# A block of self-attention, cross-attention and feed-forward: rotated heads stored with features outermost, second scores one head later

## The chip, the cores and the metric

The kernel runs on one core of one Trainium2 chip. The metric is the device time of one execution in microseconds (us), smaller is better. The times are medians of several executions; a profiled execution has its own time, which stands beside its span (first to last instruction).

## The reference

Sixteen sequences of 256 positions with 512 features pass through one block, all in float32, with 16 heads of 32 features:

```python
xn = _adaln(x, noise_emb, ln1_w, ln1_b)              # layer norm, scaled and shifted by cond
q, k, v = jnp.split(xn @ qkv_w.T, 3, axis=-1)
q, k = _rope(q...), _rope(k...)                      # halves (t1, t2) of each head's 32 features
x = x + _attn(q, k, v) @ sa_out_w.T                  # self-attention
xn = _adaln(x, noise_emb, ln2_w, ln2_b)
q = _rope(xn @ q_w.T); k = _rope(context @ k_w.T); v = context @ v_w.T
x = x + _attn(q, k, v) @ ca_out_w.T                  # cross-attention on 256 context rows
xn = _adaln(x, noise_emb, ln3_w, ln3_b)
x = x + gelu(xn @ ffn_w1.T + ffn_b1) @ ffn_w2.T + ffn_b2    # 512 -> 2048 -> 512
```

## The kernel before

**Work.** An item is one sequence in one attention layer: items 0 to 15 are the self-attention, 16 to 31 the cross-attention. An item has 16 heads, so 512 heads follow one another; after them comes the feed-forward part, which the change doesn't touch. To keep float32 accuracy every operand of a big product is split in a rounded high part (ScalarE, for weights L673) and the rest as a low part (VectorE, L817), and a product is three products (hi by hi, hi by low, low by hi), accumulated in PSUM.

**The list of steps.** `stage_order` writes one list of steps. Every engine walks through the same list in the same order and does its share of each step, so a step's place is its place on all five engines at once, SyncE's DMA issues included. A head has three places; head n begins at place 3n, item i at p = 48i. At head n stand the scores of head n, then at the second place the second scores (`weigh`) of head n - LAG, then at the third the step `total` of head n. Projections, transposes, spills and stacks for the items ahead are put at fixed places between them.

**One head.** TensorE forms the scores [query, key] (L615); VectorE takes the row maxima (L861); ScalarE takes exp with that maximum as its bias and sums each row (`total`, L744). For each group G of 8 heads ScalarE then takes the logarithm of the sums, VectorE subtracts it from the negated maxima and splits the result in two parts (`max_split`, L869 to L874), TensorE turns these (`max_turn`, L622), ScalarE copies them out of PSUM (L725), and a DMA on ScalarE's queue (`max_rows`, L734) writes them as two more rows under the stacked q. The second scores (`weigh`, L634) are formed the other way round, [key, query], over 98 rows, the last two with these constants, so that a plain exp (L758) gives weights that are already normalized. `mix` (L649) multiplies them by v, with 32 matmuls for 8 heads.

**Heads before they are used.** The projection (L605) gives 128 rows of q or k with the two halves beside each other in one PSUM bank; VectorE (L832, L836), GpSimd (L931, L932), ScalarE (`rope_high`, L719) and GpSimd (`rope_low`, L938) rotate and split them. `spill` (L994, L996) writes the high and the low part to a tensor `turned` in HBM, `stack` reads them back for four heads at a time (a quad) so that the features of high and low parts lie on the partitions: q as high, low and high once more (L1007, L1009), k as high twice and low (L1013 twice, L1015). There are six quad slots (`NQ`); a stack waits until the second scores of the slot's last quad are done (L1004). A spill waits for the stacks that read the same half of `turned` two items before.

**Other limits.** Five PSUM banks (`NS`) serve scores, second scores, turned maxima and mixes in turn; each is free when the engine named in `scores_left` has read it. Three banks serve the projections. `ctx_load` (L985) brings the context of an item of the second layer into `xT`, `ctx_split` (L713 on ScalarE, L925 on GpSimd) splits it. Weights come in 128-row chunks through four raw slots (L980).

## Time and profile before

| | |
|---|---|
| median of 3 runs | 1929.85 us (1921.75 to 1933.32) |
| profiled execution | 1925.28 us |
| its span | 1923.5 us |
| TensorE busy | 1869.4 us, 97% of the span |
| ScalarE, VectorE, GpSimd busy | 1383.3, 1294.9, 785.8 us |
| mean granted TensorE clock | 0.994 |
| DMA queue of SyncE | 304.47 MB in 304528 packets |

The attention layers fill the span up to about 1240 us, the feed-forward part the rest. Busy time says how long an engine had an instruction under way; what a change can gain is in the idle time of the engine that is always wanted, in the stretches at the lower clock, and in what each wait was ended by.

### The profile page before, as it was taken

To read this page: it belongs to the slowest core of one execution; us is meant where nothing else is said; L and a number is where in the kernel's file an instruction comes from. 1 tells how busy PE (TensorE), PEld (TensorE's weight loads), DVE (VectorE), ACT (ScalarE), POOL (GpSimd) and SP (SyncE) were. 2 spreads that over 40 slices of the span, in tenths; PEclk is the share of its full clock that TensorE was granted. 3 is DMA by queue.
4 is the path that set the end of the run, shared out by engine and by line. 5 is a ranking of instruction groups with operands and counts; after the bars stand their busy time and mean duration, and the time that the engine had idled before them with its cause. 6 is when DMAs were issued, how large, how long until landed. Compare 5 with 4: busy or idle time off the path is not lost. (4 is left out here: it accounts for less than half of the span.)

```text
span 1923.5 us, 39339 instructions
## 1 busy us (share of the span) xinstructions
PE 1869.4 (97%) x13460; PEld 1630.4 (85%) x13460; DVE 1294.9 (67%) x2250; ACT 1383.3 (72%) x3813; POOL 785.8 (41%) x818
## 2 busy tenths in 40 slices
PE   8899999999998999999999998899999999999999
PEld 7788888888877888888888886688898998989898
DVE  7766676767776677676776776446667666666754
ACT  4777777888876888888888888655666666565654
POOL 3534433443442454454454441013536354444531
PEclk9999999999998999999999999999999999999999
DMA  7666676566576778767668677343232322323130
GB/s 232 195 203 185 204 223 194 177 200 198 165 220 189 204 212 233 201 197 227 199 200 225 198 217 190 109 137 110 78 99 67 99 88 89 95 71 110 45 99 33
DMA packets 306451, 308.37 MB, mean 160 GB/s; under 512 B 21072, under 2 KB 260048, under 8 KB 306256
## 3 DMA queue, kind: packets, MB, share of 16 engines
q1 hardware_dynamic: 304528, 304.47, 53.4%
q8 instruction: 111, 1.82, 0.4%
q10 hardware_dynamic: 1728, 1.39, 0.3%
q14 instruction: 84, 0.69, 0.1%
HBM read 212.46 MB, written 92.27 MB: 158 GB/s over the span
## 5 line engine op out<-in xcount | busy, mean ns | idle before, releaser
L744 ACT ACTIVATE ps_s<-ps_s,neg_max 128x256 f32<-128x256 f32 x1024 | 452.8, 443 | 55.4 <-DVE neg_max L861 48.3
L861 DVE TENSOR_REDUCE neg_max<-ps_s 128x2 f32<-128x512 f32 x512 | 349.3, 687 | 212.8 <-PE ps_s L615 212.4
L758 ACT ACTIVATE prob<-ps_s 128x512 f32<-128x512 f32 x512 | 303.4, 593 | 137.2 <-PE ps_s L634 134.3
L634 PE MATMUL ps_s<-qT,kT 98*128 98x256 f32 x1024 | 211.6, 289 | 24.4 <-DMA qT<-max_rows 21.8
L931 POOL TENSOR_TENSOR rope_c<-rope_c,rope_s 128x256 f32<-128x256 f32 x128 | 98.4, 769 | 330.5 <-DVE rope_s L836 330.5
L615 PE MATMUL ps_s<-kT,qT 96*128 96x256 f32 x1024 | 216.5, 293 | 10.7 <-ACT ps_s L744 8.3
L615 PEld LDWEIGHTS ps_s<-kT,qT 96*128 96x128 f32 x1024 | 169.9, 190 | 60.3 <-ACT ps_s L744 28.4
L605 PE MATMUL ps_g<-xx_hi,w_hi 128*128 128x256 f32 x1024 | 208.1, 285 | 1.4 <-issue 1.4
L634 PEld LDWEIGHTS ps_s<-qT,kT 98*128 98x128 f32 x1024 | 169.3, 191 | 46.9 <-issue 21.0
L744 ACT ACTIVATION_READ_ACCUMULATOR ps_s<-ps_s,neg_max 128x1 f32 x1024 | 207.8, 203 | 0.0
L605 PE MATMUL ps_g<-xx_lo,w_hi 128*128 128x256 f32 x1024 | 205.5, 282 | 0.0
L605 PE MATMUL ps_g<-xx_hi,w_lo 128*128 128x256 f32 x1024 | 205.4, 282 | 0.0
L1297 PE MATMUL ps_y<-w_hi,h_hi 128*128 128x512 f32 x512 | 201.4, 393 | 1.2 <-DVE h_lo L1422 1.2
L1297 PE MATMUL ps_y<-w_lo,h_hi 128*128 128x512 f32 x512 | 200.7, 392 | 0.0
L1297 PE MATMUL ps_y<-w_hi,h_lo 128*128 128x512 f32 x512 | 199.3, 389 | 0.0
L1422 DVE TENSOR_TENSOR h_lo<-h_sb,h_hi 128x512 fp32r<-128x512 f32 x128 | 111.1, 872 | 104.9 <-ACT h_hi L1320 103.6
L938 POOL TENSOR_TENSOR rot_lo<-rope_c,rot_hi 128x512 fp32r<-128x512 f32 x128 | 165.6, 1295 | 16.8 <-ACT rot_hi L719 14.9
L919 POOL TENSOR_TENSOR xx_lo<-xT,xx_hi 128x512 fp32r<-128x512 f32 x66 | 86.9, 1318 | 207.3 <-ACT xx_hi L705 207.2
L1281 PE MATMUL ps_h<-xf_hi,cw_hi 128*128 128x256 f32 x592 | 167.5, 283 | 0.0
L1281 PE MATMUL ps_h<-xf_lo,cw_hi 128*128 128x256 f32 x592 | 165.8, 280 | 0.0
L1281 PE MATMUL ps_h<-xf_hi,cw_lo 128*128 128x256 f32 x592 | 165.7, 280 | 0.0
L605 PEld LDWEIGHTS ps_g<-xx_hi,w_hi 128*128 128x128 f32 x1024 | 158.5, 190 | 2.6 <-issue 1.5
(155 smaller groups left out, 4654.7 us busy)
## 6 DMA issues: line engine op xcount, KB each, us to landing
kT<-k_turned SPq DMA_DIRECT2D x384, 128.0 KB, 3.1
qT<-q_turned SPq DMA_DIRECT2D x128, 256.0 KB, 3.9
f_raw<-in_w1T SPq DMA_DIRECT2D x124, 256.0 KB, 3.1
k_turned<-rot_hi SPq DMA_DIRECT2D x64, 256.0 KB, 3.2
k_turned<-rot_lo SPq DMA_DIRECT2D x64, 256.0 KB, 2.5
q_turned<-rot_hi SPq DMA_DIRECT2D x64, 256.0 KB, 3.6
q_turned<-rot_lo SPq DMA_DIRECT2D x64, 256.0 KB, 4.1
qT<-q_turned SPq DMA_DIRECT2D x128, 128.0 KB, 3.9
```

Of the source, the lines that this page charges most:

```text
L605: ins = eng.matmul(ps_g[:, b, s * L:(s + 1) * L], w[:, row, (T * s + t) * P:(T * s + t + 1) * P], a[:, c, :], start=c == 0 and j == 0 and ...
L615: ins = eng.matmul(ps_s[:, score_bank(step), t * L:(t + 1) * L], qT[0:ROWS, quad % NQ, j, t * P:(t + 1) * P], kT[0:ROWS, quad % NQ, j, :], ...
L634: ins = eng.matmul(ps_s[:, score_bank(step), t * L:(t + 1) * L], kT[:, quad % NQ, j, t * P:(t + 1) * P], qT[:, quad % NQ, j, :], start=Tru ...
L744: ins = eng.activation(scores[:, t * L:(t + 1) * L], scores[:, t * L:(t + 1) * L], ACT.Exp, bias=neg_max[G % 2][:, t, j:j + 1], accum_out= ...
L758: eng.activation(prob[:, n % NP, :, :].rearrange("p t l -> p (t l)"), ps_s[:, score_bank(step), :], ACT.Exp).then_inc(exp_done, 1)
L861: eng.tensor_reduce(neg_max[G % 2][:, :, j], ps_s[:, score_bank(step), :].rearrange("p (t l) -> p t l", l=L), AX.X, ALU.max, negate=True). ...
L919: eng.tensor_tensor(lo[:, ks, :], xT[:, ks, :], hi[:, ks, :].bitcast(F32), ALU.subtract).then_inc(x_low_done, 1)
L931: eng.tensor_tensor(rope_c[n % 2][:, 0, :], rope_c[n % 2][:, 0, :], rope_s[:, 0, :], ALU.subtract)
L938: eng.tensor_tensor(rot_lo[:, n % NT, :, :], rope_c[n % 2][:, :, :], rot_hi[:, n % NT, :, :].bitcast(F32), ALU.subtract).then_inc(rot_lo_d ...
L1281: ins = eng.matmul(ps_h[:, bank(p, n), 0:L], w[:, cols], x_[:, k, :], start=n in OPENS and k == 0 and j == 0, stop=k == 1 and j == 2, skip ...
L1297: ins = eng.matmul(ps_y[:, t, :], h[:, t * P:(t + 1) * P], w, start=c == 0 and j == 0, stop=c == FC - 1 and j == 2)
L1422: eng.tensor_tensor(h_lo[a % NH][:, :], h_sb[a % 2][:, :], h_hi[a % NH][:, :].bitcast(F32), ALU.subtract).then_inc(h_lo_done, 1)
```

## The change

- `turned` has the order (item parity, half of the heads, high or low part, feature, head, position), so that four heads of one feature are 4 KB in one piece. The weights of q and k are laid out for it when they are split: column (half of the heads, half of the features, feature, head) with the head fastest (`by_halves`), and the tables of cosines and sines follow (`np.repeat`). Heads are so taken in another order: head n holds the features from `feature_of(n)`, which the mix reads from v and the rows of the output weights are loaded by (four DMAs of 32 rows where one had 128).
- `stack` reads a quad with two DMAs for q and two for k (three before), of 4 KB pieces.
- Second scores come 14 heads behind the scores (`LAG`), with mix and its splits. The chain that feeds them (`log` to `max_rows`) stays where it was.
- Later places: `rope_high` by 1, stack k by 2 and stack q by 1, `ctx_load` by 8 for items 18 to 31, six of the early pieces of the feed-forward part by 2 to 3 (one half of them).

```diff
--- before.py
+++ after.py
@@ -19,7 +19,7 @@
 KC = 4
 T = 2
 
-LAG = 13
+LAG = 14
 
 WARM_START, WARM_X = 14, 14
 
@@ -69,7 +69,7 @@
 
     def turns(last):
         for step, place in last.items():
-            put(place + 5, "rope_high", *step[1:])
+            put(place + 6, "rope_high", *step[1:])
             put(place + 7, "rope_low", *step[1:])
             put(place + 7, "spill", *step[1:])
 
@@ -102,7 +102,7 @@
                 put(x_place + 4 + 3 * half, "x_low", ahead, half)
         if ahead < N:
             if ahead >= B:
-                put(p - 10, "ctx_load", ahead)
+                put(p - (2 if ahead > B + 1 else 10), "ctx_load", ahead)
                 put(p + 9, "ctx_split", ahead)
             k, q, v = (project(m, ahead, 0) + project(m, ahead, 1) for m in "kqv")
             if ahead in (1, 2):
@@ -133,7 +133,7 @@
             for c in range(KC - 1):
                 spread(p + (73, 91, 98)[c], 6, [("project", "o", i, t, c) for t in range(T)])
         if i == N - 1:
-            for j, begins in enumerate(((-4, 1, 43), (24, 32, 67))):
+            for j, begins in enumerate(((-1, 3, 46), (24, 32, 67))):
                 for c in range(NE):
                     put(p + begins[c], "early", c, j)
         if i == 0:
@@ -152,8 +152,8 @@
         for n, kind in ((24, "log"), (25, "max_split"), (turn, "max_turn"), (turn + 1, "max_copy"), (turn + 2, "max_rows")):
             put(24 * G + n, kind, G)
     for quad in range(2, 4 * N):
-        put(12 * quad - 20, "stack", "k", quad)
-        put(12 * quad - 17, "stack", "q", quad)
+        put(12 * quad - 18, "stack", "k", quad)
+        put(12 * quad - 16, "stack", "q", quad)
 
     for G in range(2 * N):
         place = 3 * (8 * G + LAG + 8) + 2
@@ -265,6 +265,10 @@
     MROWS = ROWS + 2
     N_ITEMS = 2 * B
 
+    def feature_of(n):
+
+        return (T * (n % HG) + n // HG) * HD
+
     order = list(stage_order(B))
     kinds = {}
 
@@ -299,7 +303,7 @@
             slot = step[3]
         else:
             continue
-        slot_loads[slot] += 1
+        slot_loads[slot] += OH if step[0] == "w_load" and step[2] == "o" else 1
         raw_turn[step] = (slot, slot_loads[slot])
 
     raw_before, held = {}, {}
@@ -325,7 +329,7 @@
     with ExitStack() as whole:
 
 
-        turned = {m: nc.dram_tensor(f"{m}_turned", (2, D, 2, L), F32, kind="Internal").ap() for m in "qk"}
+        turned = {m: nc.dram_tensor(f"{m}_turned", (2, T, 2, HD, HG, L), F32, kind="Internal").ap() for m in "qk"}
 
         def sem(name):
             return whole.enter_context(nc.semaphore(name))
@@ -420,7 +424,7 @@
             stack_in = {m: [sem(f"stack_{m}{n}") for n in range(4)] for m in "qk"}
             max_rows_in = [sem(f"max_rows_in{n}") for n in range(2)]
 
-            STACKS = {"q": 2, "k": 3}
+            STACKS = {"q": 2, "k": 2}
 
             mod_done, mod_turned, x_turned, product_done, scores_done, max_turned, weigh_done, mix_done, rows_used = (
                 sem(n) for n in ("mod_done", "mod_turned", "x_turned", "product_done", "scores_done",
@@ -447,7 +451,7 @@
 
                 if m not in ("q", "k"):
                     return w[:, row, :]
-                return w[:, row, :].rearrange("p (s h d) -> p h s d", s=2, d=HALF)
+                return w[:, row, :].rearrange("p (u d h) -> p h u d", u=2 * T, d=HALF)
 
             def bank(step):
                 return bank_turn[step] % NB
@@ -602,7 +606,7 @@
                                                  start=c == 0 and j == 0, stop=c == KC - 1 and j == 2)
                                 continue
                             for s in range(2):
-                                ins = eng.matmul(ps_g[:, b, s * L:(s + 1) * L], w[:, row, (T * s + t) * P:(T * s + t + 1) * P], a[:, c, :],
+                                ins = eng.matmul(ps_g[:, b, s * L:(s + 1) * L], w[:, row, (2 * t + s) * P:(2 * t + s + 1) * P], a[:, c, :],
                                                  start=c == 0 and j == 0 and s == 0, stop=c == KC - 1 and j == 2, skip_group_check=True)
                         ins.then_inc(product_done if c == KC - 1 else rows_used, 1)
                     elif kind == "scores":
@@ -647,7 +651,7 @@
                                 for j in range(OH):
                                     n = OH * (KC * i + c) + j
                                     ins = eng.matmul(ps_s[j * HD:(j + 1) * HD, b, cols],
-                                                     v_sb[i % NV][:, k, c * P + j * HD:c * P + (j + 1) * HD],
+                                                     v_sb[i % NV][:, k, feature_of(n % H):feature_of(n % H) + HD],
                                                      prob[:, n % NP, k, :], start=k == 0, stop=k == T - 1)
                             ins.then_inc(mix_done, 1)
 
@@ -976,6 +980,11 @@
                             eng.wait_ge(*left)
                         if layer == "ffn":
                             eng.dma_start(hidden_view(m, w_raw[:, slot, :]), hidden_row(m)).then_inc(raw_in[slot], 16)
+                        elif m == "o":
+                            for j in range(OH):
+                                first = feature_of(OH * c + j)
+                                eng.dma_start(w_raw[j * HD:(j + 1) * HD, slot, :],
+                                              attnT[layer, MATS.index(m), first:first + HD, :]).then_inc(raw_in[slot], 16)
                         else:
                             eng.dma_start(w_raw[:, slot, :],
                                           attnT[layer, MATS.index(m), c * P:(c + 1) * P, :]).then_inc(raw_in[slot], 16)
@@ -989,11 +998,11 @@
                         if i >= 2:
                             for quad in (2 * t, 2 * t + 1):
                                 eng.wait_ge(stack_in[m][quad], 16 * STACKS[m] * (i - 1))
-                        out_to = turned[m][i % 2, T * t * P:T * (t + 1) * P].rearrange("(p d) s l -> s p d l", d=2)
+                        high, low = (turned[m][i % 2, t, part].rearrange("(s d) h l -> (d h) s l", s=2) for part in range(2))
                         eng.wait_ge(rot_hi_done, n)
-                        eng.dma_start(out_to[0], rot_hi[:, n % NT, :, :].bitcast(F32)).then_inc(spilled[m][t], 16)
+                        eng.dma_start(high, rot_hi[:, n % NT, :, :].bitcast(F32)).then_inc(spilled[m][t], 16)
                         eng.wait_ge(rot_lo_done, n)
-                        eng.dma_start(out_to[1], rot_lo[:, n % NT, :, :].bitcast(F32)).then_inc(spilled[m][t], 16)
+                        eng.dma_start(low, rot_lo[:, n % NT, :, :].bitcast(F32)).then_inc(spilled[m][t], 16)
                     elif kind == "b1_load":
                         eng.dma_start(b1_sb[:, :], b1).then_inc(b1_in, 16)
                     elif kind == "stack":
@@ -1002,18 +1011,12 @@
                         eng.wait_ge(spilled[m][n // 2], 32 * (i + 1))
                         if quad >= NQ:
                             eng.wait_ge(weigh_done, OH * (quad - NQ + 1))
-                        heads = turned[m][i % 2][n * OH * HD:(n + 1) * OH * HD]
-                        if m == "q":
-                            eng.dma_start(qT[0:2 * HD, quad % NQ, :, :].bitcast(F32),
-                                          heads.rearrange("(h d) s l -> (d s) h l", d=HD)).then_inc(stack_in[m][n], 16)
-                            eng.dma_start(qT[2 * HD:ROWS, quad % NQ, :, :].bitcast(F32),
-                                          heads[:, 0].rearrange("(h d) l -> d h l", d=HD)).then_inc(stack_in[m][n], 16)
-                        else:
-                            for s in range(2):
-                                eng.dma_start(kT[s:2 * HD:2, quad % NQ, :, :].bitcast(F32),
-                                              heads[:, 0].rearrange("(h d) l -> d h l", d=HD)).then_inc(stack_in[m][n], 16)
-                            eng.dma_start(kT[2 * HD:ROWS, quad % NQ, :, :].bitcast(F32),
-                                          heads[:, 1].rearrange("(h d) l -> d h l", d=HD)).then_inc(stack_in[m][n], 16)
+                        first = n % 2 * OH
+                        both = turned[m][i % 2, n // 2, :, :, first:first + OH, :].rearrange("s d j l -> (s d) (j l)")
+                        into = (qT if m == "q" else kT)[:, quad % NQ, :, :].rearrange("p h l -> p (h l)").bitcast(F32)
+                        pair, once = (slice(HD, ROWS), slice(0, HD)) if m == "q" else (slice(0, 2 * HD), slice(2 * HD, ROWS))
+                        eng.dma_start(into[pair, :], both).then_inc(stack_in[m][n], 16)
+                        eng.dma_start(into[once, :], both[0:HD, :]).then_inc(stack_in[m][n], 16)
                     elif kind == "res_load":
                         i = step[1]
                         layer, b = divmod(i, B)
@@ -1621,7 +1624,7 @@
 def rope_tables(length, half):
 
     inv_freq = (1.0 / np.float32(ROPE_BASE) ** (np.arange(half, dtype=np.float32) / np.float32(half))).astype(np.float32)
-    ang = np.arange(length, dtype=np.float32)[None, :] * np.tile(inv_freq, P // half)[:, None]
+    ang = np.arange(length, dtype=np.float32)[None, :] * np.repeat(inv_freq, P // half)[:, None]
     by = (2 * half) ** -0.25
     return (np.cos(ang) * by).astype(np.float32), (np.sin(ang) * by).astype(np.float32)
```

## Rows read from the trace of the kernel before

**Rows 1.** The page: TensorE's busy time and share, instructions.

```profile
PE 1869.4 (97%) x13460; PEld 1630.4 (85%) x13460; DVE 1294.9 (67%) x2250; ACT 1383.3 (72%) x3813; POOL 785.8 (41%) x818
```

**Rows 2.** Windows: busy us (instructions) by engine, PEclk, DMA share, GB/s.

```profile
640.00:1140.00 500.00, 499.64 (x3976) 438.82 (x3976) 351.13 (x663) 420.02 (x1323) 232.99 (x238) 1.00 0.73 211
...
104.00:112.00 8.00, 5.59 (x51) 3.92 (x50) 2.13 (x5) 3.56 (x12) 1.90 (x4) 0.79 0.34 111
574.00:582.00 8.00, 5.69 (x45) 3.29 (x43) 4.62 (x7) 5.91 (x18) 2.26 (x2) 0.79 1.06 284
596.00:606.00 10.00, 4.03 (x20) 3.02 (x24) 8.28 (x13) 7.03 (x21) 7.39 (x6) 0.61 0.76 206
1178.00:1186.00 8.00, 4.02 (x39) 2.41 (x38) 3.02 (x6) 4.44 (x15) 1.27 (x1) 0.79 0.72 161
```

**Rows 3.** Waits of TensorE in the whole span: us, times, longest.

```profile
PE ps_s L634 <- DMA qT<-max_rows: 21.8, 14, 4.0
PE ps_s L615 <- ACT ps_s L744: 8.3, 17, 2.2
```

**Rows 4.** The same waits between 120 and 560 us.

```profile
PE ps_s L634 <- DMA qT<-max_rows: 6.4, 6, 1.8
```

**Rows 5.** Timeline of TensorE at the second group: start, us, what, [idle].

```profile
86.87 0.47 PE L634 MATMUL ps_s<-qT,kT 98*128 98x256 f32 x2 [1.74 <-DMA qT<-max_rows]
...
87.71 1.93 PE L649 MATMUL ps_s<-prob,v_kept 128*32 128x256 f32 x32
...
90.62 0.40 PE L634 MATMUL ps_s<-qT,kT 98*128 98x256 f32 x2
```

**Rows 6.** Timeline: the four longest waits for max_rows and what follows.

```profile
107.06 0.77 PE L634 MATMUL ps_s<-qT,kT 98*128 98x256 f32 x2 [2.41 <-DMA qT<-max_rows]
...
576.95 0.47 PE L634 MATMUL ps_s<-qT,kT 98*128 98x256 f32 x2 [2.31 <-DMA qT<-max_rows]
...
605.16 0.77 PE L634 MATMUL ps_s<-qT,kT 98*128 98x256 f32 x2 [2.83 <-DMA qT<-max_rows]
...
610.00 0.40 PE L634 MATMUL ps_s<-qT,kT 98*128 98x256 f32 x2
...
1175.77 0.65 ACTq L734 DMA_DIRECT2D qT<-max_rows  x1
...
1182.08 0.77 PE L634 MATMUL ps_s<-qT,kT 98*128 98x256 f32 x2 [3.98 <-DMA qT<-max_rows]
```

**Rows 7.** The line of ctx_load between 640 and 1140 us.

```profile
DMA to landing us min/median/max: 4.8/5.7/7.1
```

**Rows 8.** Timeline of SyncE, ScalarE and TensorE at one item of layer two.

```profile
864.97 0.51 SPq L985 DMA_DIRECT2D xT<-in_ctxT  x1
...
871.21 0.60 SPq L1009 DMA_DIRECT2D qT<-q_turned  x1
...
875.75 1.15 ACT L713 ACTIVATE xx_hi<-xT 128x512 fp32r<-128x512 f32 x2
...
878.08 0.22 ACT L744 ACTIVATION_READ_ACCUMULATOR ps_s<-ps_s,neg_max 128x1 f32 x1
...
880.33 0.40 PE L634 MATMUL ps_s<-qT,kT 98*128 98x256 f32 x2
```

**Rows 9.** Timeline of SyncE and ScalarE at the first output weights.

```profile
69.93 1.53 SPq L980 DMA_DIRECT2D w_raw<-in_attnT  x2
...
73.95 0.63 ACT L673 ACTIVATE w_hi<-w_raw 128x512 fp32r<-128x512 f32 x1 [2.85 <-DMA w_raw<-in_attnT]
```

**Rows 10.** The line of a strided read on VectorE: ns min/median/max.

```profile
L806 DVE TENSOR_REDUCE gb<-ps_g x6: 418/425/426, 12.6 to 331.4; 128x64 f32<-128x256 f32 x6
```

**Rows 11.** The line that splits weights on VectorE, the same columns.

```profile
L817 DVE TENSOR_TENSOR w_lo<-w_raw,w_hi x36: 674/683/1783, 14.9 to 1190.2; 128x512 fp32r<-128x512 f32 x36
```

**Rows 12.** The page: SyncE's DMA queue.

```profile
q1 hardware_dynamic: 304528, 304.47, 53.4%
```

**Rows 13.** Timeline of ScalarE at the end of the attention.

```profile
1232.81 1.57 ACT L758 ACTIVATE prob<-ps_s 128x512 f32<-128x512 f32 x3 [0.34 <-PE ps_s L634]
```

## The prediction

> **What bounds the kernel now.** I read the page first, for the engine that is always wanted: TensorE, under way for 97% of the span [rows 1]. All that the change touches lies in the attention, so I then cut the attention in windows, to see where TensorE is not busy and where its clock was lower. Between 640 and 1140 us, most of the cross-attention, it is idle for 0.4 us in 500 [rows 2]: nothing can be gained there, only lost. The idle time lies before and after, and the view of TensorE's waits says by whom it ends: 21.8 us in 14 waits of the second scores for the DMA that brings the maxima and logarithms under the stacked q, and 8.3 us in 17 short waits of the first scores for ScalarE to leave a PSUM bank [rows 3]. The reader is to see that the large wait is a distance in the list of steps: the first second scores of a group stand a little over two heads behind the copy that feeds their DMA, and the DMA lands later than that in 14 groups of 64.
>
> The third thing is the clock. In four windows around the longest waits the granted clock was 0.79, 0.79, 0.61 and 0.79 [rows 2], which is a mix of the full level, 2.4 GHz, and the half one, 1.2 GHz; in each TensorE stood still for 2.3 to 4.0 us before or beside it [rows 6]. At these means the windows lose 8 x 0.21 = 1.7 us (three times) and 10 x 0.39 = 3.9 us, together 9.0 us. So 21.8 + 8.3 + 9.0, some 39 us or 2% of the span, is all that the change can reach.
>
> **LAG from 13 to 14.** The second scores move behind by one head while log, turn, copy and DMA stay. No instruction is added. How much later TensorE comes to the first second scores of a group is read from the list of what lies between them and the next ones: in the second group 90.62 - 86.87 = 3.75 us, of which mix, which moves with them, is 1.93 [rows 5]. That leaves 1.8 us, against a wait of 1.74: gone. The six waits between 120 and 560 us are 6.4 us in all, none over 1.8 [rows 4], so all of these go as well, and the others below 1.8 with them. Of the four longest [rows 6] something is left:
> - at 107.06: 2.41 - 1.9 = 0.5 us; at 576.95: 2.31 - 1.9 = 0.4 us;
> - at 605.16: the next second scores come 4.84 us later, but at the half clock; at the full one that is 2.4 to 3, less 1.93 for mix, so the new head gives 0.5 to 1.1 us, taken as 1.0, and 1.8 us stay;
> - at 1182.08: no projection stands between heads here, only a turn of x and one pair of scores. I estimate 1.2 us, between nothing and the 1.8 of the full heads; of 3.98 us 2.8 stay. The DMA itself took 1182.08 - 1175.77 = 6.3 us, which is what makes this one long.
>
> Left over 5.5, recovered 21.8 - 5.5 = **16.3 us**, with 13 and 19 as bounds.
>
> **The clock.** Where a wait falls from 2.4 or 2.3 to 0.5 us the drop behind it should go: 2 x 1.7 = 3.4 us. The third one stands in a cluster where ScalarE and the weight loads are late too; I take 1.5 of its 3.9 us. The last one stays. **4.9 us**, from 0 to 9.0.
>
> **Stacks and spills.** The same bytes are read in a quarter of the pieces. No view splits the queue by piece size; the queue as a whole took 53.4% of 16 engines for 304528 packets [rows 12], which is 0.534 x 16 x 1923.5 / 304528 = 54 ns for a packet of 1 KB in the mean. If the longer pieces saved nothing of that, the DMA load stays at 0.73 in the cross-attention [rows 2]; if all of it was a cost per packet, it would fall by a third. TensorE waits for no stack, so this is worth only what it takes off the landings of the short DMA; I take 0.5 us off the waits left over (0 to 3). One of three k DMAs goes, and with it about 0.6 us of SyncE's queue a quad (an issue of the q stack takes 0.60 [rows 8]); SyncE is a late engine only at the start and around 600 us.
>
> The Trainium skill speaks against a gain here: its page "DMA: Bandwidth & Descriptors", section Specifications, puts the least transfer for line rate at 512 B, and the old pieces are 1 KB already. By that rule the 0.5 would be nothing and the sum 19.9; the row of the queue can't decide it.
>
> **Stacks and rounding later.** Stack k and q move 2 and 1 places, but SyncE stood before the stack waiting for the slot's last second scores anyway, and these come 3 places later. From there to the first scores of the quad 20 places of the list remain, over six heads, at about 1.8 us or more a head 11 us at least; a stack is issued in about 2.5 us and landed in a few more. Cost nothing; if that cover were gone TensorE would wait for a stack, of which there is no row. `rope_high` one place later delays a spill by under a microsecond against heads that are wanted tens of places on: nothing.
>
> **ctx_load later.** This is the dangerous piece, as it lies in the stretch without idle time. At the item of rows 8 SyncE issues it at 864.97, and ScalarE wants it at 875.75. In the new list it stands behind the stack of q, whose last issue is at 871.21 for 0.60 us; with one k DMA fewer it goes out at about 871.2. It lands in 4.8 to 7.1 us, median 5.7 [rows 7], so at 876.9 (876.0 to 878.3), which is **1.2 us late** (0.3 to 2.6). ScalarE is in order: queued behind it are the exp of the second scores and the `total` of that head, and TensorE waits for the banks of both. The `total` ends at 878.08 + 0.22 = 878.30 and TensorE takes its bank at 880.33 [rows 8]: cover 2.0 us. I put the cost at nothing; past 2.0 us of lateness each microsecond costs 14 (items 18 to 31).
>
> **Weights in a new order.** ScalarE and VectorE write 16 rows of q and k weights with 32 bytes from element to element instead of in runs of 16. The nearest row is a reduction on VectorE that reads 256 elements with long strides in 425 ns [rows 10]; half of the 683 ns that a split of 512 elements takes [rows 11] is 342, and 83 ns more is a fixed part rather than a price of strides. I take nothing; the upper bound is double time for each split. What covers it is little: at the start four of them stand before the first q projection, and eight stand around 600 us.
>
> The output weights of the first layer come by four DMAs a row instead of one. In the old list two of them were issued at 69.93 and ScalarE stood 2.85 us for the first at 73.95 [rows 9], with a few TensorE waits behind it. Three more issues of about 0.6 us are 1.8 us, against about as much saved on the k stacks ahead of it in the same queue. **+0.8 us** (-1 to +3).
>
> **The tail.** One more head of second scores runs when no scores are left to fill the time; it goes at ScalarE's pace there, 1.57 us for three [rows 13]. **+0.5 us** (0 to 1.5); the early feed-forward pieces move along.
>
> **The sum.** 16.3 + 4.9 + 0.5 - 0.8 - 0.5 = 20.4 us faster. Against the profiled execution, 1923.5 of span and 1.8 around it, that is 1904.9; this execution lay 4.6 us under the median of the runs shown, and the forecast goes by the median: 1929.85 - 20.4 = **1909.5 us**. One per cent of the median, about what can be told from no change, is 19.3 us, so the forecast lies just beyond it.
>
> **The rivals.**
> - *Something else is late next.* With the waits for the maxima gone, TensorE comes earlier to the banks; ScalarE is 84% busy (420.02 of 500 us) and the 17 waits for it [rows 3] grow. The 14 waits were partly time in which ScalarE caught up. For it speak the clusters around 600 and 1180 us, where both are late; against it the stretch at 640 to 1140, where nothing waits although ScalarE is as busy. It would leave half the gain: 1920.
> - *The context lands late.* Its 512 KB now queue behind a low spill and four stack transfers, 1 MB issued in the 4 us before it, instead of behind a residual. If that makes the landing 9.3 us instead of 5.7, it is 4.8 late and 2.8 beyond the cover, and GpSimd's half of the split follows it: 14 x 2.8 = 39 us, 1909.5 + 39 = 1948, slower. It decides from a landing of 6.6 us on (the 5.7 and the 0.8 of cover that 1.2 us of lateness leave), and 7.1 was seen; at a landing of 7.9 us it costs 19 and the change is worth nothing.
> - *Strides cost.* ScalarE and VectorE write a split in double time. At the start four VectorE splits add 0.68 each, 2.7 us, and around 600 us eight add 8 x (0.63 + 0.68) = 10 us to two late engines, of which I let half show: 8 us, 1917. The skill has a rule that would do this (page "SBUF — State Buffer", Door 1: accesses that go to a new 16-byte line each time pay a penalty).
> - *The cluster around 600 us dissolves.* In the new list the last load of value weights goes before a stack, not behind it. If that takes ScalarE's waits for weights away, and the last drop of the clock goes too, another 12 us: 1897.
>
> **How the numbers follow.** The forecast has 0.50, of which 0.37 beyond 1% faster; something else late next 0.18; context late 0.15, two thirds of it beyond 1% slower; strides 0.07; the cluster dissolved 0.10. Faster by over 1% is 0.37 + 0.10 = 0.47, slower 0.10, within 0.43. The range, 1893 to 1932, leaves out most of the late context and the best of the last case; the forecast's own is 1900 to 1917.
>
> **What the next profile would show.** LAG: waits for max_rows between 4 and 7 us in all, none between 120 and 560. Clock: full in the first two of the four windows. Context: TensorE's idle time between 640 and 1140 still under 2 us, with ScalarE waiting about 1 us before each L713 of items 18 to 31; tens of microseconds of idle time there would be the second rival. Stacks: longer packets and a share of the queue below 53.4%; no TensorE wait for them. Strides: the two split lines at 0.63 and 0.68 us. The prediction is wrong if ScalarE's waits grow by what the maxima's shrink, or if the landing of that short DMA itself gets longer behind long pieces.

## The result and the profile after

The changed kernel takes 1935.38 us (median of 11 runs, 1932.97 to 1948.72) against 1929.85 us before (median of 11 in the same session). The medians are 5.5 us apart, 0.29%; the ratio over all executions, which goes by more than the middle ones, is 1.0046, 95% interval 1.0032 to 1.006 (the means, 1937.5 and 1928.9, are 8.6 us apart). The loss is less than the 1% set as the bound of no change, but measurably slower. Forecast were 1909.5 us, and the range ended at 1932. The profiled execution took 1935.38 us, its span 1933.6; the granted clock was 0.995 in the mean, 0.994 before.

The page of the changed kernel, TensorE's busy time and SyncE's DMA queue:

```profile
PE 1882.0 (97%) x13460; PEld 1628.2 (84%) x13460; DVE 1313.9 (68%) x2250; ACT 1388.6 (72%) x3813; POOL 786.4 (41%) x818
...
q1 hardware_dynamic: 229136, 304.46, 51.7%
```

TensorE's instructions are as many as in [rows 1] and its clock the same, yet its busy time grew by 12.6 us. Matmul ends are modelled, so short waits for a PSUM bank can be counted as busy; that sum must be kept in mind beside the next view. VectorE's busy time grew by 19.0 us and ScalarE's by 5.3, with as many instructions.

TensorE's waits after, to be laid beside [rows 3] (L638 here is L634 there, L619 is L615, L748 is L744):

```profile
PE ps_s L638 <- ACT ps_s L748: 11.9, 17, 1.7
PE ps_s L619 <- ACT ps_s L748: 11.1, 23, 2.4
PE ps_s L638 <- DMA qT<-max_rows: 3.9, 5, 1.8
```

The wait that the forecast wanted gone went: 21.8 us fell to 3.9. ScalarE's lateness took its place in the view: of the first scores' banks 8.3 us became 11.1, and the second scores' banks, with three waits of 1.9 us in all before, now stand first with 11.9. Waits for ScalarE have grown by 12.8 us where the maxima's shrank by 17.9, which is most of the way to the first of the forecast's own signs of being wrong.

Windows of the changed kernel, the columns as in [rows 2]:

```profile
640.00:1140.00 500.00, 494.18 (x3876) 426.34 (x3875) 353.44 (x652) 410.52 (x1293) 228.47 (x235) 1.00 0.69 206
...
104.00:112.00 8.00, 6.70 (x56) 6.22 (x58) 6.12 (x12) 5.90 (x19) 2.66 (x4) 1.00 0.76 191
574.00:582.00 8.00, 6.37 (x35) 5.15 (x33) 6.81 (x8) 7.75 (x21) 6.64 (x5) 1.00 0.63 177
...
1178.00:1186.00 8.00, 7.96 (x66) 5.67 (x65) 6.97 (x11) 7.19 (x24) 1.26 (x1) 1.00 1.01 315
...
596.00:606.00 10.00, 5.61 (x27) 4.32 (x26) 10.00 (x16) 9.34 (x25) 6.97 (x5) 0.69 0.68 205
...
298.00:306.00 8.00, 6.23 (x55) 3.99 (x54) 4.44 (x8) 3.68 (x14) 3.36 (x4) 0.80 0.86 270
```

The three short windows have the full clock now. The cluster at 600 us does not: 0.69, and VectorE is busy for all ten of its microseconds. The last line is a drop that the kernel before doesn't have (it has 1.00 in that window). The first line is the bad one. In the stretch that had 0.4 us of idle time in 500, TensorE is now idle for 5.8 us, and it gets through 100 of its 3976 matmuls fewer, 2.5% or some 12.6 us of work by an estimate from these counts: more than half of what is lost in this stretch doesn't show as idle time. Its largest waits here:

```profile
PE ps_s L638 <- ACT ps_s L748: 4.8, 7, 1.7
```

The timeline of one cross-attention item shows what sits there (SyncE's issues, ScalarE, TensorE):

```profile
881.14 0.42 SPq L994 DMA_DIRECT2D xT<-in_ctxT  x1
...
889.00 1.15 ACT L717 ACTIVATE xx_hi<-xT 128x512 fp32r<-128x512 f32 x2 [3.70 <-DMA xT<-in_ctxT]
...
891.60 0.50 PE L638 MATMUL ps_s<-qT,kT 98*128 98x256 f32 x2 [1.68 <-ACT ps_s L748]
```

This is the latest of them, landed after 7.8 us. ScalarE stands 3.70 us for the context, and TensorE then waits 1.68 us for a bank that ScalarE should have emptied. The line of ctx_load between 640 and 1140 us, who waited for it, and its landing, beside [rows 7]:

```profile
  ACT xx_hi L717: 29.9, 14
...
DMA to landing us min/median/max: 5.5/6.1/7.8
```

Fourteen items, 29.9 us of ScalarE. Last, the lines that split the weights of q and k, of which [rows 11] is the old VectorE one (ns, min/median/max):

```profile
L677 ACT ACTIVATE w_hi<-v_sb x2: 1228/1258/1289, 20.1 to 21.0; 128x512 fp32r<-128x512 f32 x2
L677 ACT ACTIVATE w_hi<-v_kept x2: 1344/1359/1374, 22.0 to 23.0; 128x512 fp32r<-128x512 f32 x2
...
L821 DVE TENSOR_TENSOR w_lo<-v_sb,w_hi x2: 1169/1190/1210, 22.3 to 23.4; 128x512 fp32r<-128x512 f32 x2
L821 DVE TENSOR_TENSOR w_lo<-v_kept,w_hi x2: 1146/1172/1197, 24.5 to 25.6; 128x512 fp32r<-128x512 f32 x2
```

These four loads, of q's rows, are written in the new order, and each split takes about twice its time (ScalarE) or 1.7 times (VectorE).

### The profile page after: what moved, and what is told of

Its sections match the earlier page's. It is cut to its first block and busy times, and to the rows that moved or that the text cites. A ratio compares the mean times of both kernels' runs of the same rounds, so it can differ in the third digit from the quotient of the medians.

```text
span 1933.6 us, 39235 instructions
## 1 busy us (share of the span) xinstructions
PE 1882.0 (97%) x13460; PEld 1628.2 (84%) x13460; DVE 1313.9 (68%) x2250; ACT 1388.6 (72%) x3813; POOL 786.4 (41%) x818
## 3 DMA queue, kind: packets, MB, share of 16 engines
q1 hardware_dynamic: 229136, 304.46, 51.7%
## 5 line engine op out<-in xcount | busy, mean ns | idle before, releaser
L748 ACT ACTIVATE ps_s<-ps_s,neg_max 128x256 f32<-128x256 f32 x1024 | 457.1, 448 | 77.5 <-DVE neg_max L865 68.2
L619 PE MATMUL ps_s<-kT,qT 96*128 96x256 f32 x1024 | 220.0, 296 | 14.6 <-ACT ps_s L748 11.1
L638 PE MATMUL ps_s<-qT,kT 98*128 98x256 f32 x1024 | 213.9, 291 | 16.2 <-ACT ps_s L748 11.9
L619 PEld LDWEIGHTS ps_s<-kT,qT 96*128 96x128 f32 x1024 | 167.5, 190 | 65.9 <-issue 26.7
L748 ACT ACTIVATION_READ_ACCUMULATOR ps_s<-ps_s,neg_max 128x1 f32 x1024 | 211.0, 206 | 0.0
L638 PEld LDWEIGHTS ps_s<-qT,kT 98*128 98x128 f32 x1024 | 167.9, 191 | 45.7 <-ACT ps_s L748 24.7
L609 PEld LDWEIGHTS ps_g<-xx_lo,w_hi 128*128 128x128 f32 x1024 | 158.5, 190 | 0.0
```

The source lines that it names most:

```text
L609: ins = eng.matmul(ps_g[:, b, s * L:(s + 1) * L], w[:, row, (2 * t + s) * P:(2 * t + s + 1) * P], a[:, c, :], start=c == 0 and j == 0 and ...
L619: ins = eng.matmul(ps_s[:, score_bank(step), t * L:(t + 1) * L], qT[0:ROWS, quad % NQ, j, t * P:(t + 1) * P], kT[0:ROWS, quad % NQ, j, :], ...
L638: ins = eng.matmul(ps_s[:, score_bank(step), t * L:(t + 1) * L], kT[:, quad % NQ, j, t * P:(t + 1) * P], qT[:, quad % NQ, j, :], start=Tru ...
L748: ins = eng.activation(scores[:, t * L:(t + 1) * L], scores[:, t * L:(t + 1) * L], ACT.Exp, bias=neg_max[G % 2][:, t, j:j + 1], accum_out= ...
```

## The experiments

All times are medians; the ratio is to the kernel before on the same chip, with its 95% interval. The kernel before had 1928.99 us beside the first four runs, 1929.3 beside the next four and 1928.8 beside the last four. The ratios are taken over all executions, so they can differ by one or two thousandths from what two medians give, and each interval is 2 to 4 us wide to either side: a difference between two runs of some 3 us or less is not told from nothing.

| run | us | ratio |
|---|---|---|
| 1. changed kernel, context early | 1928.23 | 1.0002 (0.9987 to 1.0017) |
| 2. before + LAG 14 | 1924.78 | 0.9978 (0.9965 to 0.999) |
| 3. changed kernel, layout alone | 1933.84 | 1.0026 (1.0012 to 1.004) |
| 4. changed kernel, weights ready in the new order | 1931.25 | 1.0011 (0.9994 to 1.0028) |
| 5. before + LAG 14, o_low earlier | 1916.07 | 0.9938 (0.9916 to 0.996) |
| 6. before + maxima turned earlier | 1916.42 | 0.9944 (0.9926 to 0.9962) |
| 7. changed kernel, context early, weights ready | 1927.24 | 0.9993 (0.998 to 1.0006) |
| 8. the same, o_low earlier | 1915.20 | 0.9937 (0.9917 to 0.9957) |
| 9. before + context late | 1933.79 | 1.0025 (1.0006 to 1.0043) |
| 10. before + o_low earlier | 1929.76 | 1.0005 (0.9988 to 1.0022) |
| 11. before + LAG 14, o_low earlier, maxima earlier | 1915.83 | 0.9927 (0.9906 to 0.9947) |
| 12. changed kernel, context early, weights ready, o_low and maxima earlier | 1910.43 | 0.9903 (0.9881 to 0.9924) |

An "item" below is one (layer, batch) of 16 heads. Its length is read between the starts of its first scores and the next item's. Items 2, 8 and 11 of the kernel before, where nothing waits, have 36.1 us (452.60 to 488.69 for the last), nearly all of the cross-attention 35.7.

**1. The context early again, all else as changed.**

```
-                put(p - (2 if ahead > B + 1 else 10), "ctx_load", ahead)
+                put(p - 10, "ctx_load", ahead)
```

> The changed kernel with ctx_load back at place p - 10 for all items. Theory 1 (the late context is what ate the gain of LAG): ScalarE no longer stands before the context split (it stood 1.3 to 3.7 us in each of 14 items), the cross-attention items go back from 36.1 to 37.9 us towards 35.7, and the kernel is 8 to 12 us faster than the changed one, near 1926. Theory 2 (ScalarE's backlog comes from the second scores at their new place, the context wait was covered by banks): under 3 us faster, items stay at 36.1 or more.

1928.23 us, 7.2 less than the changed kernel (8.5 by the two ratios). TensorE's waits between 640 and 1140 us:

```profile
PE ps_s L638 <- ACT ps_s L748: 1.0, 2, 0.7
```

and the landing of the 14 contexts in the same stretch:

```profile
DMA to landing us min/median/max: 6.2/6.7/8.6
```

The second scores' waits for ScalarE in this stretch fall from 4.8 us to 1.0, and ScalarE no longer stands before L717. From item 16 to item 30 this kernel is 6.1 us shorter than the changed one (1156.7 - 653.6 against 1166.6 - 657.4). With the late context undone the changed kernel is no longer slower than before, but the change is still worth nothing. The landing is longer here, 6.7 us in the middle against 6.1 in the changed kernel, so going out behind the stacks did not lengthen it: the context was late because it was issued late.

**2. LAG alone.**

```
-LAG = 13
+LAG = 14
```

> The kernel before with LAG = 14 and nothing else. Theory 1: the waits for max_rows fall from 21.8 to about 5 us as they did in the changed kernel, and the time falls with them, by 12 to 18 us, to near 1915. Theory 2 (a wait for banks takes the place of each wait for the maxima): waits for max_rows fall as much, waits for ScalarE grow by as much, and the time stays within 5 us of before.

1924.78 us. Its waits and its busy time:

```profile
PE 1875.0 (98%) x13460; PEld 1626.6 (85%) x13460; DVE 1301.5 (68%) x2250; ACT 1386.3 (72%) x3813; POOL 784.9 (41%) x818
```

```profile
PE ps_s L615 <- ACT ps_s L744: 10.4, 23, 2.1
PE ps_s L634 <- ACT ps_s L744: 5.5, 10, 1.1
PE ps_s L634 <- DMA qT<-max_rows: 4.4, 3, 2.3
PE ps_s L615 <- DMA qT<-q_turned: 2.3, 1, 2.3
```

17.4 us of waits for the maxima went and 4 us of time. ScalarE's banks took back 5.7 us of it, waits for a q stack 1.6 (2.3 against 0.7 before), and 5.6 more hide in the busy time. The loss is regular: each self-attention item without a wait for maxima is 36.5 us long instead of 36.1, each of the cross-attention 36.0 instead of 35.7. The extra time is lost at the item's first heads. There the timeline of LAG 14 (VectorE, ScalarE and TensorE after a mix) has

```profile
444.48 0.60 ACT L766 ACTIVATE o_hi<-ps_s 128x512 fp32r<-128x512 f32 x1 [0.29 <-PE ps_s L649]
...
447.15 0.68 DVE L836 TENSOR_TENSOR rope_s<-ps_g,sin_sb 128x512 f32<-128x512 f32 x1
...
447.75 0.68 DVE L880 TENSOR_TENSOR o_lo<-ps_s,o_hi 128x512 fp32r<-128x512 f32 x1
...
448.48 0.51 PE L615 MATMUL ps_s<-kT,qT 96*128 96x256 f32 x2
...
449.06 0.45 ACT L744 ACTIVATE ps_s<-ps_s,neg_max 128x256 f32<-128x256 f32 x1 [0.73 <-DVE neg_max L861]
```

where the kernel before had

```profile
448.81 0.60 ACT L766 ACTIVATE o_hi<-ps_s 128x512 fp32r<-128x512 f32 x1 [0.92 <-PE ps_s L649]
...
450.42 0.67 DVE L880 TENSOR_TENSOR o_lo<-ps_s,o_hi 128x512 fp32r<-128x512 f32 x1
```

The reader is to look at the distance from `o_hi` to `o_lo`: 1.6 us before, 3.3 now. `o_low` is what returns the mix's PSUM bank. One head later in the list it stands behind a rope step, which waits for a projection of TensorE; VectorE is in order, so the bank comes back late, first scores want it at that moment, and ScalarE stands 0.73 us before the `total` behind them. The view of the waits of TensorE's weight loads (PEld) shows a part of what the busy time hides:

```profile
PEld ps_s L615 <- DVE o_lo L880: 3.6, 13, 0.3
```

In the kernel before that view has `o_lo` for 1.5 us in two waits. That became the next theory.

**3. The layout alone**: the changed kernel with LAG and all places in the list as before.

```
-LAG = 14
+LAG = 13
...
-            put(place + 6, "rope_high", *step[1:])
+            put(place + 5, "rope_high", *step[1:])
...
-                put(p - (2 if ahead > B + 1 else 10), "ctx_load", ahead)
+                put(p - 10, "ctx_load", ahead)
...
-        put(12 * quad - 18, "stack", "k", quad)
-        put(12 * quad - 16, "stack", "q", quad)
+        put(12 * quad - 20, "stack", "k", quad)
+        put(12 * quad - 17, "stack", "q", quad)
```

The early feed-forward pieces that moved (three of the six) go back too.

> The changed kernel with every place and LAG as before: only the layout, the 4 KB stacks, the order of heads, the strided weight splits and the four DMAs a row of output weights are left. Theory 1: the strided splits cost 3 us at the start and some around 600 us, the long pieces give nothing to speak of: 3 to 8 us slower than before. Theory 2 (the long pieces help the short DMA of the maxima): waits for max_rows well under 21.8 us, time at or under before. If neither: a loss above 10 us would put the whole result on the layout.

1933.84 us, 4.9 more than before. The first of the first scores start at

```profile
44.28 0.42 PE L619 MATMUL ps_s<-kT,qT 96*128 96x256 f32 x2
```

and at 41.29 in the kernel before, so 3.0 of it are lost at the start; nearly all cross-attention items have 35.7 us, as before. The waits for the maxima:

```profile
PE ps_s L638 <- DMA qT<-max_rows: 19.5, 11, 3.3
```

That is no more than the 21.8 in 14 before. The landing of this short DMA has no row of its own; by these waits the long pieces made it neither longer, which was the forecast's second sign of being wrong, nor much shorter, which was theory 2. The long pieces bring no time where nothing waits for them.

**4. The weights ready in the new order.** The q and k weights come to the kernel reordered in DRAM, so that it leaves the reordering out, and both splits write runs of neighbours again.

```
-                return w[:, row, :].rearrange("p (u d h) -> p h u d", u=2 * T, d=HALF)
+                return w[:, row, :]
```

> The changed kernel with the q and k weights already in the new column order in HBM (reordered before the launch), so that the splits write element beside element. Theory 1: splits back to 0.63 us on ScalarE and 0.68 on VectorE (1.2 to 1.37 and 1.15 to 1.2 for the strided ones), first scores 3 us earlier, 3 to 6 us faster than the changed kernel. Theory 2 (the start is late for another reason, the issues of the output weights or the stacks): splits short again, start unchanged, under 1.5 us.

1931.25 us, 4.1 less than the changed kernel. The split of the same rows, and the first scores:

```profile
L677 ACT ACTIVATE w_hi<-v_sb x2: 627/630/632, 19.2 to 19.7; 128x512 fp32r<-128x512 f32 x2
...
L821 DVE TENSOR_TENSOR w_lo<-v_sb,w_hi x2: 680/680/681, 21.3 to 21.9; 128x512 fp32r<-128x512 f32 x2
...
41.48 0.40 PE L619 MATMUL ps_s<-kT,qT 96*128 96x256 f32 x2
```

The changed kernel's first scores start at 44.36 us; with the same loads, issues and stacks they are here 2.9 us earlier. The strides are the cost at the start. Of the layout's 4.9 us (run 3) they would be 4.1, but that size is loose: it is taken with the context late, and run 7 gives another. The 0.8 left over is as much as the forecast put on the four DMAs for a row of output weights, but it is less than these intervals can tell.

**5. LAG 14 with o_low one place earlier.** It tests the theory of run 2.

```
-        for n, kind in enumerate(("mix", "o_split", "o_low")):
+        for n, kind in ((0, "mix"), (1, "o_split"), (1, "o_low")):
```

> The kernel before with LAG 14 and with o_low one place of the list earlier, at the place of o_split. With LAG 14 alone each self-attention item without a wait for maxima had become 0.4 us longer, lost at its first heads, where VectorE's o_low had come to stand behind a rope step that waits for TensorE, so that the bank of the mix was returned late. Theory: that order is the cause. Items of self-attention fall back from 36.5 to about 36.1 us, TensorE's waits of the first scores for ScalarE from 10.4 to about 8 us, and the time is 4 to 6 us below LAG 14 alone, near 1919. Rival (the second scores come nearer to the exponentials of the first scores on ScalarE, whatever VectorE does): items stay at 36.5 us and the time stays at 1925.

1916.07 us, 8.7 below LAG 14 alone and more than the theory asked for. After the same mix, and from the first scores of item 11 to those of item 12:

```profile
445.93 0.60 ACT L766 ACTIVATE o_hi<-ps_s 128x512 fp32r<-128x512 f32 x1 [0.29 <-PE ps_s L649]
...
446.94 0.68 DVE L880 TENSOR_TENSOR o_lo<-ps_s,o_hi 128x512 fp32r<-128x512 f32 x1
...
447.79 0.40 PE L615 MATMUL ps_s<-kT,qT 96*128 96x256 f32 x2
...
483.86 0.40 PE L615 MATMUL ps_s<-kT,qT 96*128 96x256 f32 x2
```

`o_lo` comes 1.0 us behind `o_hi`, and the item is 36.1 us long again; the ones of the cross-attention are 35.7. TensorE's busy time is 1866.9 us, 8.1 less than with LAG 14 alone, and its weight loads for the first scores have no wait for `o_lo` left. Its waits:

```profile
PE ps_s L634 <- DMA qT<-max_rows: 10.4, 7, 2.4
PE ps_s L615 <- ACT ps_s L744: 8.4, 18, 2.2
PE ps_s L634 <- ACT ps_s L744: 5.7, 10, 1.3
```

The waits for maxima are larger than with LAG 14 alone (10.4 against 4.4). TensorE coming earlier would do that, but it isn't shown: the profiles with LAG 14 and the turn in its old place have 3.9 (changed kernel), 5.0, 4.4, 9.0, 10.4, 6.0 and 7.7 us (runs 1, 2, 4, 5, 7, 8), in no clear order. The first scores' waits are back at [rows 3]'s 8.3. The rival, that ScalarE's exps cause them, falls for the regular part. The second scores' 5.7 us stay: that part of it stands.

**6. The maxima two places earlier, LAG 13.**

```
-        turn = 32 if G < 2 * B else 30
+        turn = 30
```

> The kernel before, LAG 13, with the three steps that turn, copy and spill the maxima of a group two places of the list earlier in the first layer (place 30 instead of 32, as the second layer has it). It gives the short DMA about as much more time as a later LAG does, without moving the second scores, the mix or the output split. Theory (LAG's gain is the waits for maxima, its price is what moves with the second scores): the six waits between 120 and 560 us go, the self-attention items without a wait stay at 36.1 us, waits for maxima fall from 21.8 to about 12 us, and the time is 5 to 8 us below before, near 1922. Rival (whatever takes the waits away, ScalarE is late next and TensorE waits for its banks instead): the first scores' waits for ScalarE grow by as much as the maxima's shrink, and the time is that of before.

1916.42 us. The waits:

```profile
PE ps_s L634 <- DMA qT<-max_rows: 11.4, 9, 2.3
PE ps_s L622 <- DVE max_parts L874: 6.8, 14, 0.9
PE ps_s L615 <- ACT ps_s L744: 6.6, 8, 2.5
```

It gives 12.9 us by moving three steps instead of everything behind the second scores. That is more than the 5 to 8 us expected; the two profiles, which the waits are read from, are 8.1 us apart (spans of 1923.5 and 1915.4), because that of the kernel before is of one of its quicker executions. It has a price of its own: the turn now stands up to 0.9 us for VectorE's `max_parts`, and an undisturbed self-attention item has 36.3 us. The rival, that waits for ScalarE's banks grow by what the maxima's shrink, is wrong here: the first scores' fell, from 8.3 to 6.6.

**7 and 8. Both costs of the changed kernel undone, and then o_low earlier**: the edits of 1 and 4, and in the second run that of 5.

> The changed kernel with the two costs undone that runs have shown alone: ctx_load at p - 10 in all items, and the weights of q and k laid out in the new order in DRAM, so that both splits write runs of neighbours. If the costs add (7.2 us for the context, 4.1 for the strided splits), the time is 1935.4 - 11.3 = 1924; it is LAG 14 with longer DMA pieces and nothing else. Rival (both costs hide the same idle time): 1928, that of the early context alone.

> As the run with both costs undone, and o_low one place earlier, at the place of o_split. If the order of o_low is what LAG 14 costs in each self-attention item, this is 4 to 6 us faster than the run without it, 1918 to 1920, and faster than both kernels. Rival: no difference from the run without it.

1927.24 and 1915.20 us. The two costs don't add up fully: each alone gives 7.2 and 4.1, both together 8.1 of 11.3, a gap of about what the intervals leave open. The first run is one microsecond under the early context alone, nearer to its rival than to the sum, so the strides are worth 1.0 us here and 4.1 in run 4, though the first scores come 2.8 us earlier here too (41.92 against 44.72). With o_low earlier come 12 us more, the same step as from run 2 to run 5 and larger; all quiet items go from 36.5 to 36.1 and from 36.0 to 35.7.

**9. The context late, all else as before.** It asks whether the long pieces or LAG 14 are needed for the cost of run 1.

```
-                put(p - 10, "ctx_load", ahead)
+                put(p - (2 if ahead > B + 1 else 10), "ctx_load", ahead)
```

> The kernel before, with only ctx_load moved from place p - 10 to p - 2 for items 18 to 31: short pieces, LAG 13. Theory: the place behind the stacks makes the context late, whatever the pieces and LAG; ScalarE stands 1 to 4 us before its half of the split in 14 items, which become 0.3 to 2 us longer each, together 5 to 9 us, and the time is near 1936. Rival A: the long pieces of the stacks hold the queue, so that here the landing stays at 6 us and the cost is under 1 us, 1930. Rival B: LAG 14 had used up the cover (TensorE comes nearer to ScalarE's total), so that here the waits of ScalarE are there but TensorE waits for under 3 us in all, 1931.

1933.79 us, 5.0 more than before. One item, SyncE, ScalarE and TensorE:

```profile
737.16 0.43 SPq L985 DMA_DIRECT2D xT<-in_ctxT  x1
...
742.66 1.16 ACT L713 ACTIVATE xx_hi<-xT 128x512 fp32r<-128x512 f32 x2 [3.59 <-DMA xT<-in_ctxT]
...
745.26 0.50 PE L634 MATMUL ps_s<-qT,kT 98*128 98x256 f32 x2 [1.58 <-ACT ps_s L744]
```

and the landing of all 14:

```profile
DMA to landing us min/median/max: 5.0/5.3/6.9
```

Both rivals fall: short pieces and LAG 13 have the cost as well. It is the place in SyncE's order. The landings are no longer than in the kernel before (5.3 against 5.7 in the middle). This item took 5.5; it is the latest of the 14 because it was issued only 1.9 us before ScalarE stood for it (742.66 - 3.59 - 737.16), where the changed kernel had some 4.15. Here ScalarE is 3.59 us late and TensorE 1.58; in the changed kernel 3.70 and 1.68. The difference, 2.0 us both times, is the cover that the forecast worked out from [rows 8].

**10. o_low earlier, LAG 13**, the control of run 5, with the same edit.

> The kernel before, LAG 13, with only o_low one place earlier. It is a control: with LAG 13 o_low ran ahead of the rope step already, so if that order is all that the edit changes, items stay at 36.1 and 35.7 us and the time is that of before within 2 us. Rival: the edit gains 8 us by itself, whatever LAG is.

1929.76 us, no difference. The edit is worth something only where LAG 14 has put the step behind the rope.

**11 and 12. The best of all.** Run 5 with the edit of run 6, and run 8 with it.

> The kernel before with LAG 14, o_low one place earlier, and the maxima turned two places earlier in the first layer. Waits for maxima were 10.4 us in 7 with the first two edits and 11.4 us in 9 with the last alone; if the two ways add their time, under 5 us of them are left and the items 3 to 7, now 37.7 to 38.7, don't change otherwise. Theory (waits add): 1911. Rival (with 2 us of slack in hand already the second way gives nothing more, or its steps on VectorE come in the way of the first scores): 1915 to 1917.

> The changed kernel with the context early, the weights laid out in the new order in DRAM, o_low one place earlier and the maxima turned two places earlier in the first layer. Against the same without the last edit (1915.2): under 3 us of waits for maxima left of 7.7, so 1911 to 1913 if the time follows the waits; 1915 if something else is late next. Against the run on the old layout it shows what the long pieces are worth: nothing, if both come out alike.

1915.83 and 1910.43 us. In run 11 no wait for the maxima stands in the view any more, and the time is that of runs 5 and 6; something else is late next, its rival:

```profile
PE ps_s L634 <- ACT ps_s L744: 10.9, 10, 2.7
PE ps_s L622 <- DVE max_parts L874: 7.4, 15, 0.9
```

Run 12, on the new layout, is the fastest of all kernels here, 1.0% under before. Its waits:

```profile
PE ps_s L619 <- ACT ps_s L748: 8.7, 8, 2.2
PE ps_s L626 <- DVE max_parts L878: 7.7, 16, 0.9
```

Between it and run 11 lie 5.4 us. The intervals of the ratios overlap (0.9906 to 0.9947 and 0.9881 to 0.9924), but five of its six executions are under the quickest of run 11 (1913.38), so the two did not come out alike. Runs 8 and 5, on the same two layouts, differ by 0.9. The long pieces, the two DMAs for k and the later places of the spills and stacks all lie between runs 11 and 12, and no run takes them apart: whether the long pieces are worth anything is left open.

## Why the prediction was wrong

**LAG, waits for the maxima: right, with some luck.** 5.5 us were to be left, 3.9 are, with 1.8 as the longest. But that is the lowest of seven profiles with the same distance (up to 10.4 in run 5), and between 120 and 560 us, where none was to be left, the changed kernel kept one of 1.8, LAG 14 alone one of 1.1 and run 5 three of 3.8 in all.

**LAG, its price: the step that failed.** The forecast took 16.3 us of waits as 16.3 us of time with "No instruction is added". It counted what the mix takes of TensorE and never walked `o_split` and `o_low`, which move with it, through VectorE's list. There `o_low` fell behind a rope step: 0.4 us in each self-attention item and 0.3 in each of the cross-attention. Undone, by one place in the list, it is worth 8.7 us alone and 12 on the new layout, and LAG's gain is 13.2 us instead of 4.2 (runs 2, 5, 8; 10 as the control). That is still 7.5 short of the 20.7 that LAG, the clock and the tail were to bring. Run 5 shows three things it can lie in and doesn't price them apart: 10.4 us of waits for the maxima are left and not 5.5, second scores' waits for ScalarE went from 1.9 to 5.7 us, and the waits for q stacks from 0.7 to 3.7. The second is what the first rival named, with "half the gain" and 0.18.

**The clock: two windows right, and their gain not seen in the whole.** Of the four windows three are at 1.00, one more than forecast. The cluster at 600 us stays lowered, 0.69, where 1.5 us were to come back; over the wider stretch from 585 to 625 us the clock is 0.83 and was 0.87, so it got longer, and the rival that it dissolves is out. A new drop stands at 303 us, beside a wait of 1.8 us for the maxima, in an item that is 41.7 us long and was 39.0. Run 7 has it too (0.79 from 298 to 306 us, an item of 42.1), run 1 has not (1.00, 39.9). The mean over the span went from 0.994 to 0.995, which on 1930 us is some 2 us and not 4.9. (The windows are fixed in time, and the work in them is another after a gain or a loss of some microseconds.)

**The context: the mechanism right, the size taken at its middle.** Issued 4.15 us ahead of its use instead of the forecast 4.55, landed in 6.1 us instead of 5.7, it is late by 2.0 us in the middle of 14 items (1.3 to 3.7) instead of 1.2. The cover of 2.0 us was right to 0.1. The failed step is "I put the cost at nothing": its own bounds for the lateness, 0.3 to 2.6, already passed the cover, and only the part of each item beyond it counts, so a spread of landings and issues costs even where the middle one costs nothing. Seven of the 14 were past it. TensorE's second scores waited 4.8 us for ScalarE between 640 and 1140, and in time it is 7.2 us (run 1), or 5.0 on the old kernel (run 9). The rival *the context lands late* had named the place, at 39 us and 0.15, but not the cause: it wanted a longer landing behind the stacks, and the landing is shorter there than at the old place, 6.1 us against 6.7 on the new layout (run 1) and 5.3 against 5.7 on the old one (run 9).

**The strides: taken at nothing, each split measured near the upper bound.** ScalarE's splits of q's rows went from about 630 to between 1228 and 1374 ns, VectorE's from 680 to between 1146 and 1210. The first scores are 2.9 us late by it, where the rival had 2.7; the whole cost is 4.1 us with the context late (run 4) and 1.0 with it early (run 7 against run 1). The row chosen as the nearest, a strided read of a reduction, [rows 10], says nothing of strided writes. The Trainium skill had the right sign (page "SBUF — State Buffer", Door 1, the penalty for going to a new 16-byte line each time); it was given 0.07. Of the 8 us that the rival let show, some 5 of them at 600 us, hardly anything was there beyond the start: at most 1.2 us are left for all other places, and the granted clock between 585 and 625 us is 0.83 with strides and without (runs 4 and 7).

**Stacks, rope later, the tail: nothing seen.** The queue's share fell from 53.4% to 51.7%, its packets by a quarter and not by the third that the forecast's bound took. No wait for a k stack appears, and the q stack's waits, 1.7 us in three, are no more than in LAG 14 alone (2.3). The 0.5 us taken off the landings is shown by no run.

**The sum.** LAG gives 4.2, the layout costs 4.9 and the context 7.2, each alone (runs 2, 3, 1): 7.9 us slower, against 5.5 between the medians and 8.6 between the means. That the three terms make up the result is shown; whether they share some of their time, as run 7 hints, the intervals leave open.

## What to carry to other kernels

When a step moves in a list of steps, walk every engine's queue for everything that moves with it, down to the small one that returns a buffer: one `o_low` behind the wrong neighbour ate two thirds of LAG's gain, and its cure was one place. To buy time for a short transfer, move what feeds it (three steps, 12.9 us) rather than all that uses it (4.2 us until mended). A cover is compared with the whole spread of what it must hide, of issue and landing, item by item, and not with the median.

## What the runs showed of the hardware

**Splits with strided writes.** 512 fp32 elements a partition written in the new order (32 bytes from element to element) took 1.23 to 1.37 us on ScalarE and 1.15 to 1.21 us on VectorE, against 0.63 and 0.68 in runs of neighbours: about twice and 1.7 times.

**Long pieces.** A quarter fewer packets (229136 for 304528) for the same bytes took 0.517 x 16 x 1933.6 = 15995 us of DMA engine time instead of 0.534 x 16 x 1923.5 = 16434: 2.7% less. That is 439 us for 75392 packets, an estimate of 6 ns for each packet saved: most of the 54 ns of a packet of 1 KB was its bytes. The landing of the context didn't gain by it: behind the stacks it took 5.3 us in the middle with short pieces (run 9) and 6.1 with long ones. Nor are long pieces alone the cause of that: at the old place it took 5.7 before, 5.5 with the layout alone (run 3) and 6.7 with LAG 14 and the later stacks as well (run 1), and which of these does it is open.

**Waits inside busy time.** With LAG 14 alone TensorE's busy time rose by 5.6 us for the same instructions and clock, and fell below that of before when the bank came back in time. Waits of some tenths of a microsecond don't all stand in the view of the matmuls' waits, which has none for `o_lo` at the first scores in run 2; the view of the weight loads (3.6 us in 13 there), the busy sum and the length of an undisturbed item show them.
